# A cross-attention block on one NeuronCore: two buffers for weight sums, three places for activation parts, another order of the norms

## What is computed

```python
B, LQ, LK, D, H, HD = 4, 512, 512, 512, 16, 32          # float32
x = layer_norm(hidden_states, ln1_w, ln1_b)
q = x @ q_w + q_b;  k = ctx @ k_w + k_b;  v = ctx @ v_w + v_b        # 16 heads of 32
attn = softmax(where(mask, q k^T / sqrt(32), min))
hidden = (attn v) @ cproj_w + cproj_b + hidden_states
y = layer_norm(hidden, ln2_w, ln2_b)
y = gelu_tanh(y @ fc_w + fc_b)          # 512 -> 2048
return hidden + y @ proj_w + proj_b     # 2048 -> 512
```

## Time and profile before

| | us |
|---|---|
| median of three runs | 834.61 (833.38 to 835.18) |
| profiled execution, own time | 833.2 |
| its span, first to last instruction | 831.4 |
| mean granted TensorE clock | 0.969 of full |

### The profile page before, as it was taken

The page is one execution under the profiler, slowest core; times in us unless marked ns, Lnnn a source line. Parts: engine busy times, 40 slices in busy tenths (PEclk is TensorE's granted clock), DMA queues, the critical chain, the costliest instruction groups (busy, mean ns, idle before and its releaser), DMA issues.

```text
span 831.4 us, 10419 instructions
## 1 busy us (share of the span) xinstructions
PE 747.7 (90%) x3568; PEld 505.1 (61%) x3568; DVE 546.7 (66%) x1077; ACT 362.2 (44%) x618; POOL 448.3 (54%) x307
## 2 busy tenths in 40 slices
PE   7999999989999999999995888987775988899998
PEld 5888876433443434444483667765554866678776
DVE  6764357788888898887846556468675236554564
ACT  4433332576665666767724344212123433432221
POOL 2724040479987887886437623534844234235673
PEclk9999999999999999999997999989977989999999
DMA  8657295867567747886173215253822512133442
GB/s 304 229 165 278 98 283 158 254 178 183 138 161 193 218 130 189 195 176 229 29 184 105 76 51 190 76 110 116 246 86 77 164 51 76 52 89 92 143 129 79
DMA packets 118196, 124.24 MB, mean 149 GB/s; under 512 B 41248, under 2 KB 66084, under 8 KB 118144
## 3 DMA queue, kind: packets, MB, share of 16 engines
q1 hardware_dynamic: 118000, 123.56, 51.8%
q10 hardware_dynamic: 144, 0.02, 0.0%
HBM read 94.05 MB, written 29.37 MB: 148 GB/s over the span
## 4 chain that ended last, share of the span: by engine, by line
PE 67%; DVE 19%; issue 4%; POOL 4%; ACT 3%; DMA 2%; SPq 2%; ACTq 0%; DVEq 0%
PE ps L588 18%; PE ps L590 17%; PE ps L589 17%; DVE ps L1278 5%; PE ps L711 4%; PE ps L695 4%; PE ps L680 3%; PE ps L726 3%; DVE BIG L1322 2%; DVE R L1481 2%; DVE R L1214 1%; POOL BIG L1595 1%; DVE HR L1391 1%; SPq L410 1%; DVE BF L1381 1%
## 5 line engine op out<-in xcount | busy, mean ns | idle before, releaser
L956 ACT ACTIVATE Pt<-ps 128x512 f32<-128x512 f32 x256 | 137.7, 598 | 71.9 <-PE ps L695 70.5
L1595 POOL TENSOR_TENSOR BIG<-RW,BIG 128x512 fp32r<-128x512 f32 x66 | 101.5, 1542 | 112.7 <-ACT BIG L1057 110.9
L588 PE MATMUL ps<-BIG,HR 128*128 128x512 f32 x256 | 105.7, 413 | 31.5 <-DVE HR L1393 28.8
L1057 ACT ACTIVATE BIG<-RW 128x512 fp32r<-128x512 f32 x64 | 40.2, 631 | 154.8 <-PE ps L590 135.1
L590 PE MATMUL ps<-BIG,HR 128*128 128x512 f32 x256 | 103.5, 404 | 0.0
L589 PE MATMUL ps<-BIG,HR 128*128 128x512 f32 x256 | 103.3, 404 | 0.0
L695 PE MATMUL ps<-BIG 98*128 98x512 f32 x256 | 93.3, 440 | 4.2 <-ACT Pt L956 3.7
L1278 DVE CUSTOM_DVE_ANT_0 ps<-ps,FU 128x512 f32<-128x512 f32 x128 | 84.6, 723 | 15.4 <-PE ps L680 15.3
L1278 DVE CUSTOM_DVE_ANT_0 ps<-ps,BIG 128x512 f32<-128x512 f32 x128 | 84.6, 724 | 10.9 <-PE ps L680 10.8
L695 PEld LDWEIGHTS ps<-BIG 98*128 98x128 f32 x256 | 44.1, 187 | 68.8 <-issue 29.6
L588 PEld LDWEIGHTS ps<-BIG,HR 128*128 128x128 f32 x256 | 50.6, 198 | 47.4 <-DVE HR L1393 33.4
(11 more groups left out here) (160 smaller groups left out, 1607.5 us busy)
## 6 DMA issues: line engine op xcount, KB each, us to landing
RW<-in_proj_w SPq DMA_DIRECT2D x64, 256.0 KB, 2.7
BIG<-qs SPq DMA_DIRECT2D x62, 256.0 KB, 2.9
BIG<-ks SPq DMA_DIRECT2D x62, 256.0 KB, 3.2
RW<-in_fc_w SPq DMA_DIRECT2D x48, 256.0 KB, 3.1
ks<-BIG SPq DMA_DIRECT2D x32, 256.0 KB, 2.0
qs<-BIG SPq DMA_DIRECT2D x32, 256.0 KB, 6.0
R<-hd SPq DMA_DIRECT2D x20, 256.0 KB, 3.9
R<-in_x SPq DMA_DIRECT2D x16, 256.0 KB, 5.5
```

Of the source, the lines that this page charges most:

```text
L588: eng.matmul(outp, a[0], b[0], start=first, stop=False, skip_group_check=onto)
L956: eng.activation(Pt[:, r, j % 2, :], bank(bank_a(("s2", i, j))), ACT.Exp, scale=SCALE).then_inc(S["a_ra"], 1)
L1057: eng.activation(second(n)[0], raw_w(at), ACT.Copy).then_inc(S["a_pj"], 1)
L1595: eng.tensor_tensor(dst, src, high.bitcast(F32), ALU.subtract).then_inc(S[name], 1)
```

## The change

Tiles: `SUMS` becomes two buffers, FU and the first half of tile R0; product m uses buffer m modulo 2, and `weight_sums(m)` waits for `rest_low(m - 2)`. The parts of activations get a third place in the second half of R0 (named RX); split n waits for pj n - 3. To make room, the last two front blocks of turn 0 lie in R1 (RY), those of turn 1 in BIG, and the rest places of turn 1 are taken in another order (`rest(q, p)`). The turned blocks 2 and 3 of batch 1 go to R0, so that they need not wait for FU.

Order: the statistics of batch 1's norm leave steps 58 to 62 of the attention and stand in front of turn 0, behind the low part of weights 2 and ahead of the last division. Its transposes come one step earlier, the low part of weights 3 behind them. In `RAW_W` the pair wr0, wr8 stands ahead of wf6 and wf7. The blocks of turn 0 are formed at p = 4 and 5 instead of 5, their high parts at p = 4 and 5, `rest_high(q, 0)` at p = 6 in both turns. DVE takes three low parts of blocks and POOL two. In the rest stage `rest_low(p + 2)` comes ahead of `add_c12(p)`, and POOL's sums run one further ahead. In pj of turn 0 the norm's steps are spread anew: statistics at n = 2 to 9, norms at 10, 11, 15, 16, transposes and stores at 12 to 19, loads at 16 and 20, affines at 19, 20, 23, 24, blocks at 25 to 28; `add_out` goes from n = 17 to 21 and 22, in halves, `store_out` to 23, `residual` to 25, `bias_add` from 21 to 28.

The diff, cut to its core and with eight spaces of indentation taken off; "@@ L" gives the line in the kernel before:

```diff
@@ L47
-R1 = sb("R1", [128, 4, 512], F32)
+with nc.sbuf_tensor("R1", [128, 4, 512], F32) as R1:
+    pass
+RY = sb("RY", [128, 2048], R)
@@ L98
-        base, off = ((RX, 0), (RX, 1024), (BIG, 18944), (BIG, 19968))[p % 4]
+        base, off = BIG, (16384, 17408, 18944, 19968)[p % 4]
@@ L101
-                     (RX, 0), (RX, 1024))[p]
+                     (RY, 0), (RY, 1024))[p]
@@ L104
-def rest(p):
+def rest(q, p):
@@ L106
-    return [BIG[:, 16384 + 2560 * (p % 3) + 1280 * h:][:, 0:1280] for h in range(2)]
+    return [BIG[:, 16384 + 2560 * ((p + 2 * q) % 3) + 1280 * h:][:, 0:1280] for h in range(2)]
@@ L112
-SUMS = FU.rearrange("p a n -> p (a n)")
+SUMS = [t.rearrange("p a n -> p (a n)") for t in (FU, R0[:, 0:2, :])]
@@ L121
+def parts_of(n):
+    return HR[:, n % 3] if n % 3 < 2 else RX[:, 1024:2048].rearrange("p (h t) -> p h t", h=2)
+
+def turned(b, c):
+    return R0[:, c % 2, :] if b == 1 and c >= 2 else FU[:, c % 2, :]
+
@@ L128
-    RAW_W += [("wf", HF * q + p, p) for p in range(HF)]
@@ L129
+        RAW_W += [("wf", HF * q + p, p)]
+        if p == 5:
+            RAW_W += [("wr", HF * q, 0), ("wr", HF * q, HF)]
+    for p in range(1, HF):
...
@@ L532
-            if p < 6 if q == 0 else p >= 4:
-                load_raw_w(first + p + (6 if q == 0 else 4))
+                load_raw_w(first + 8)
+                load_raw_w(first + 9)
+            if q == 1 and p == 3:
+                residual(2)
+            if q == 1 and 4 <= p < 6:
+                load_raw_w(first + p + 6)
+            if q == 0 and p < 6:
+                load_raw_w(first + p + 6)
+            if q == 0 and p < 2:
+                y_store(1, 2 * p)
+                y_store(1, 2 * p + 1)
@@ L535
-                y_store(1, 0)
-                y_store(1, 1)
-            if q == 0 and p == 2:
-                y_store(1, 2)
-                y_store(1, 3)
@@ L545
-            if q == 1 and p == 2:
-                residual(2)
@@ L558
-            if n + 28 < 56:
+            if n + 28 < 56 or q == 0:
@@ L560
-            elif q == 0:
-                load_raw_w(n + 28)
@@ L564
-                    if n == 8 + c:
+                    if n == 12 + c:
@@ L566
-                    if n == 17 + c:
+                    if n == 16 + c:
@@ L568
-                if n == 12:
+                if n == 16:
@@ L570
-                if n == 21:
+                if n == 20:
@@ L572
-            if n == 18:
+            if n == 23:
@@ L573
+            if n == 25:
@@ L778
-        pe.wait_ge(*(("v_yq", 2 * q + y + 1) if y < 2 else ("g_yq", 3 * q + y - 1)))
+        pe.wait_ge(*(("v_yq", 3 * q + y + 1) if y < 3 else ("g_yq", 2 * q + y - 2)))
...
@@ L996
-            act.wait_ge("v_yq", 4)
-            act.wait_ge("g_yq", 6)
+            act.wait_ge("v_yq", 6)
+            act.wait_ge("g_yq", 4)
@@ L1026
-                act.wait_ge("p_sm", NS)
+                act.wait_ge("g_al", NS)
@@ L1041
-        else:
-            act.wait_ge("p_p2", 2 * HF)
+        elif p == 0:
@@ L1044
-        hi = rest(p)[0]
+        else:
+            act.wait_ge("p_p2", HF + (6 if p == 1 else 8))
+        hi = rest(q, p)[0]
@@ L1047
-        eng.activation(hi[:, 256:1280], SUMS, ACT.Copy).then_inc(S["a_wr"], 1)
+        eng.activation(hi[:, 256:1280], SUMS[m % 2], ACT.Copy).then_inc(S["a_wr"], 1)
@@ L1054
-            act.wait_ge("p_p3", HF * (b // 2) + 6)
+            act.wait_ge("p_p3", HF * (b // 2) + (7 if b else 6))
@@ L1160
-            if q == 0 and p == 6:
-                for n in range(4):
+            if q == 0 and p == 4:
+                block_high(0, 0)
+                block_high(0, 1)
+            if q == 0 and p == 5:
+                for n in (2, 3, 4):
@@ L1163
-            if p == 6 and q:
+            if p == 6:
@@ L1165
-        if q == 0:
-            block_high(0, 4)
-            rest_high(q, 0)
@@ L1185
-                if n == 16:
-                    for k in range(4):
-                        y_high(2, k)
-                if n == 26:
-                    for j in range(4):
-                        block_high(1, j)
-                    block_high(1, 4)
+                if 20 <= n < 22:
+                    y_high(2, 2 * n - 40)
+                    y_high(2, 2 * n - 39)
+                if 27 <= n:
+                    block_high(1, n - 27)
@@ L1222
-        if c >= 2:
+        if b == 1 and c >= 2:
+            dve.wait_ge("p_sm", NS)
+        elif c >= 2:
@@ L1223
+        elif b == 2:
+            dve.wait_ge("v_wr", 2 * HF)
@@ L1229
-        eng.transpose(FU[:, c % 2, :], LN[b][:, c, :]).then_inc(S["v_yb"], 1)
+        eng.transpose(turned(b, c), LN[b][:, c, :]).then_inc(S["v_yb"], 1)
...
@@ L1324
-    def blocks(q):
+    def block(q, n):
...
@@ L1348
-            dve.wait_ge(*(("v_yq", n + 1) if n < 2 else ("g_yq", n - 1)))
+            dve.wait_ge(*(("v_yq", n + 1) if n < 3 else ("g_yq", 1)))
@@ L1358
-                dve.wait_ge("g_yq", 3)
+                dve.wait_ge("g_yq", 2)
@@ L1386
+        hi, lo = parts_of(n)[:, 0, :], parts_of(n)[:, 1, :]
@@ L1388
+        elif n >= 3:
+            dve.wait_ge("p_pr", 4 * (n - 2))
@@ L1390
-            dve.wait_ge("p_pr", 4 * (n - 1))
-        eng.tensor_copy(HR[:, n % 2, 0, :], g).then_inc(S["v_hh"], 1)
+            dve.wait_ge("p_sm", NS)
+        eng.tensor_copy(hi, g).then_inc(S["v_hh"], 1)
@@ L1393
-        eng.tensor_tensor(HR[:, n % 2, 1, :], g, HR[:, n % 2, 0, :].bitcast(F32), ALU.subtract).then_inc(S["v_hl"], 1)
+        eng.tensor_tensor(lo, g, hi.bitcast(F32), ALU.subtract).then_inc(S["v_hl"], 1)
@@ L1395
-    def add_out(b):
-        for c in range(4):
+    def add_out(b, cs):
+        for c in cs:
@@ L1469
-        if i in Y2_STATS:
-            c = Y2_STATS.index(i)
-            dve.wait_ge(f"d_h{c}", 32)
-            statistics(LN[1], 1, 5, c)
@@ L1491
-        if i == 62:
-            for c in range(4):
-                aggregate(1, 5, c)
-            variances(1, 5)
@@ L1508
-                add_out(1)
-            if q == 0 and p + 2 < HF:
-                front_low_part(0, p + 2)
+                add_out(1, range(4))
+            if q and p < 3:
+                block_low(1, p)
@@ L1513
+                front_low_part(0, 2)
+                for c in range(4):
+                    dve.wait_ge(f"d_h{c}", 32)
+                    statistics(LN[1], 1, 5, c)
+                for c in range(4):
+                    aggregate(1, 5, c)
+                variances(1, 5)
@@ L1520
-            if q == 0 and p == 1:
@@ L1523
-            if q == 0 and p == 2:
+            if q == 0 and p == 1:
@@ L1525
+                front_low_part(0, 3)
+            if q == 0 and 2 <= p < 6:
+                front_low_part(0, p + 2)
@@ L1531
-            if q == 0 and p == 4:
+            if q == 0 and p == 3:
@@ L1533
+            if q == 0 and p == 4:
+                block(0, 0)
+                block(0, 1)
@@ L1535
-                blocks(0)
+                block(0, 2)
+                block(0, 3)
@@ L1537
-                block_low(0, 0)
-                block_low(0, 1)
+                for n in range(3):
+                    block_low(0, n)
@@ L1540
-        add_u2(q, 0)
@@ L1541
+        add_u2(q, 0)
@@ L1548
-            add_c12(q, p)
@@ L1550
+            add_c12(q, p)
@@ L1560
-            if n == 17:
-                add_out(2 * q)
+            if 21 <= n < 23:
+                add_out(2 * q, (2 * n - 42, 2 * n - 41))
@@ L1563
-                for b, at in ((2, 0), (3, 9)):
-                    if 2 <= n - at < 6:
-                        c = n - at - 2
+                for b, at in ((2, 2), (3, 6)):
+                    if 0 <= n - at < 4:
+                        c = n - at
+                        if b == 3 and c == 0:
+                            for k in range(4):
+                                aggregate(0, 6, k)
+                            variances(0, 6)
@@ L1568
-                    if n - at == 5:
-                        for c in range(4):
-                            aggregate(b % 2, 4 + b, c)
-                        variances(b % 2, 4 + b)
-                    if n - at == 7:
-                        for c in range(4):
+                if n == 11:
+                    for c in range(4):
+                        aggregate(1, 7, c)
+                    variances(1, 7)
+                for b, at in ((2, 10), (3, 15)):
+                    if 0 <= n - at < 2:
+                        for c in (2 * (n - at), 2 * (n - at) + 1):
@@ L1575
-                    if 8 <= n - at < 12:
-                        y_block(b, n - at - 8)
-                    if 14 <= n - at < 16:
-                        for k in (2 * (n - at) - 28, 2 * (n - at) - 27):
+                for b, at in ((2, 12), (3, 16)):
+                    if 0 <= n - at < 4:
+                        y_block(b, n - at)
+                for b, at in ((2, 19), (3, 23)):
+                    if 0 <= n - at < 2:
+                        for k in (2 * (n - at), 2 * (n - at) + 1):
@@ L1580
-                if n == 25:
-                    blocks(1)
```

(61 more changed lines are left out.)

19 lines of the change are left out of this document (9 added, 10 removed).

## The result

| | before | after |
|---|---|---|
| median, us | 834.0 (832.16 to 835.18, 4 runs) | 811.78 (810.83 to 814.88, 4 runs) |
| ratio to before | | 0.9742 [0.9709, 0.9775] |
| profiled execution, own time / span | 833.2 / 831.4 | 814.88 / 813.1 |

22 us faster, against 38 forecast: outside the 788 to 804 of the forecast itself, inside the wider range of 780 to 815. The profiled execution of after is its slowest run; spans of the others are 809 to 810.5.

What follows compares the result with a forecast made beforehand. TensorE bounds the kernel through the attention; behind it PE stalls, mostly on DVE, in pj of turn 0. Sum: 833.2 - 0.5 + 0 - 7.4 - 28 - 2.3 = 795.0 us, median 796.4; forecast 788 to 804 (0.60), wider 780 to 815 (0.80).

Steps and rivals of the forecast that it cites:

- rival (a): DVE becomes the bound of pj in turn 0: stage 115 us instead of 101, kernel 810 us; chance 0.20.
- attention: Statistics leave DVE during the attention, whose end has 1.6 us of PE stalls: gain 0.5 us, bounds 0 and 1.6.
- front of turn 0: Two new stalls (4.3 and 1.2 us) against the 9.06 us stall shrinking to about 2: taken as 0, bounds -2 and +4.
- rest stages and second front: Shorter rest periods against later loads of wr1 and wr9, and 0.65 us at turn 1's beginning: together -7.4 us.
- pj of turn 0: Second projection of turn 0: third place and spread steps leave 14.3 us lost instead of 42.4, a gain of 28 us.
- loss 2.6 and 2.8, and 1.4 for the clock: Start of each rest stage: wr1 and wr9 wait for rest_low(0); 2.6 and 2.8 us lost, plus 1.4 in each.
- cross wait at n = 28: Near the end of pj of turn 0, front_low waits for ScalarE's step 28, which waits for pj 28's end: 5.3 us stall.
- (d): Stalls are waits within DVE's own order, so pj of turn 0 keeps its 42.4 us loss: 833 within 3; chance 0.03.
- (c): Slow turned stores on SP make weights for pj late, kernel slower than before: 845 us at 10 us a store; chance 0.02.
- (b): pj of turn 0 runs as its twin, wf6 comes in time, rest stages lose nothing at their start: 781 us; chance 0.14.
- rule on shared ports: If all 32 casts in pj of turn 0 took 2.56 us beside POOL: stage 52 us longer, kernel 848; chance 0.01.
- a pj stage over 110 us: Sign that the forecast is wrong; pj of turn 0 was expected at 96 to 106 us, turn 1 at 87 to 88.

Runs made afterwards that it cites:

- e2: The changed kernel with the raw weights loaded in the order of before (all eight wf, then the wr pairs): 792.44 us, ratio to before 0.9515.
- e1: The changed kernel with add_u2(0) moved ahead of rest_low(1) on DVE at the start of both rest stages: 807.67 us, ratio to before 0.9701.
- e9: The changed kernel with the next front's weight high parts a step earlier on ScalarE, ahead of block_high, and low parts a step later on DVE: 803.22 us, ratio 0.9659.
- e8: The changed kernel with five edits: old raw-weight order, earlier add_u2(0), earlier front low part 3, four turned-block places, next front's high parts earlier and low parts later: 780.24 us.
- e6: The changed kernel with two places for the parts of activations instead of three: ratio to before 0.9831.

## Why the prediction was right in direction and half in size

The profiled execution's span is 813.1 us where the sum had 793.2 (795.0 less 1.8 around it). The forecast itself, 788 to 804, missed. The range of 780 to 815 holds the result only because it took in a part of rival (a), whose cause is not the one that showed: that it holds is in part luck. By terms, in us of change against before:

| term | predicted | measured | off |
|---|---|---|---|
| attention | -0.5 | +1.8 | 2.3 |
| front of turn 0 | 0 | +1.6 | 1.6 |
| rest stages and second front | -7.4 | -2.1 | 5.3 |
| pj of turn 0 | -28 | -16.9 | 11.1 |
| pj of turn 1 | -2.3 | -2.8 | -0.5 |

- **Attention.** PE waits 1.6 us at its end as before. The statistics hid there. The rest of the 2.3 us is scatter: the twelve kernels of the experiments, with the same first half, reach the front at 402.3 to 403.9 us, this execution at 405.1.
- **Front.** All three stalls stood where they were predicted: 5.78 us for 4.3, 1.39 for 1.2, 1.93 for "about 2" in place of 9.06. The four norms took 2.87 us and not 1.9, and the low part behind the transposes 1.31 instead of 0.68.
- **Rest stages, the step that failed: "loss 2.6 and 2.8, and 1.4 for the clock".** The mechanism was named, that the loads of wr1 and wr9 wait for `rest_low(0)`; it was priced at 4 to 6 us a turn and cost about 10 (e2). Two terms were longer than priced in turn 0: landing 5.5 us for 3.7 to 4.6, the low part 2.27 for 1.2. One wait was not seen: `add_u2(0)` stands behind `rest_low(1)` in DVE's queue, and PE's third product needs its bank, so that 12 matmuls covered the chain, not 18 (e1). The stalls were 8.17 and 5.61 us. The gain of the stages without this, 11.3 and 9.6 us in e2, was more than the 9.4 and 7.5 stated. The bound of 0 for both stages together held; the value inside it did not.
- **pj of turn 0, the larger miss: 14.3 us predicted lost, 25.5 measured, some 23 in other executions.** By PE's timeline the 25.5 are 17.0 of stalls, where the sum had 10.5 (1.7, 3.5 and 5.3), and 8.4 of matmuls that start later than 0.227 us after the one before, where it had 3.8 (the clock 1.4 twice, and small gaps of 1). Three stretches of slow matmuls cost 3.0, 2.4 and 1.6 us, and not two of 1.4; the six of before, counted in the same way, had cost 11.7, so that 1.4 was low by the rows at hand. The cross wait at n = 28 was right in place and chain (high part of weights 31 behind the end of pj 28, block high, front high, low part, split). Its own terms give 4.55 with a split of 1.1 us and 7.65 with one of 4.2, of which 5.3 was taken; with the 1.62 us low part (1.2 predicted) and a split of 3.1 us the stall was 6.99:

```profile
614.19 1.62 DVE L1327 TENSOR_TENSOR BIG<-RW,BIG 128x512 fp32r<-128x512 f32 x1 [4.18 <-ACT BIG L1042]
615.73 1.49 DVE L1408 CAST RX<-BF 128x512 fp32r<-128x512 f32 x1
617.26 1.64 DVE L1410 TENSOR_TENSOR RX<-BF,RX 128x512 fp32r<-128x512 f32 x1
```

With the slow matmuls and the 1.82 us stall behind it the fault cost 9 to 11 us of the stage (e9). n = 20 cost 4.32 for 1.7, the transpose waiting for its place as predicted (4.82 us). The 3.5 for n = 20 to 27 was near (1.78 and 1.35 us). So the mechanisms were right; the sizes of two stalls and of the clock were not, and DVE's 120 instructions took 98.6 us where 85.9 was counted.
- **Rival (a)**, DVE as the bound and 810 us, came nearest in time. The contention that it named showed (98.6 us busy), but it did not set the stage's length: without the cross wait nearly the same DVE work (95.1 us) fits into 101. (d) is out by the stage's 17 us, (c) by its weights, which PE never waited for there. (b)'s 781 is what e8 reaches with both faults taken away and three edits more.
- **The rule on shared ports** (the Trainium skill, SBUF — State Buffer, "Who interferes with whom") was given a chance of 0.01 at its full price, since the prediction saw long casts only where POOL works without a pause. The changed kernel has them also where POOL does one low part a period, in POOL's and DVE's timelines:

```profile
535.07 1.29 POOL L1621 TENSOR_TENSOR BIG<-RW,BIG 128x512 fp32r<-128x512 f32 x1 [1.43 <-ACT BIG L1069]
...
535.20 1.45 DVE L1408 CAST HR<-BF 128x512 fp32r<-128x512 f32 x1
```

The cast starts 0.13 us into POOL's piece and ends 0.29 us behind it, where a cast with POOL idle takes 0.42. The trace agrees with the rule, by which the one that comes second waits for the whole instruction: 14 of the stage's 31 casts take over 0.6 us (0.89 to 2.59), and each of them starts inside a piece of POOL's and ends 0.28 or 0.29 us behind the end of one. The 31 casts went from 19.4 us before to 27.4, their low parts from 28.1 to 31.3; that is 11.2 of the 12.7 us. Before, 25 of the 31 took 0.38 to 0.43 us, 22 of them with POOL at rest. With two places and the new steps (e6) the casts take 21.3 us, so the third place, which lets DVE run out of step with PE, has a price too.
- What was said would show it wrong, "a pj stage over 110 us", showed (112.6; usually 110.5, just over).

## What to carry to other kernels

A further buffer covered here only delays that are not tied to the consumer's own progress: before adding one, look in the producer's queue for waits (here a root, a weight's high part) that end at a fixed distance behind the consumer, and move those first. When the order of loads is changed over a ring of places, price the first load that must now wait for a place to come free, as a whole chain to the consumer with every instruction queued behind it: here this took back nearly all that the stages had won. Take durations for a denser engine from rows in which its neighbour works, not from the shortest ones.
